# Gated slot attention on Trainium2: the first four steps of a software pipeline in another order

## The reference, cut to what matters

```python
q = _swish((x @ Wq).reshape(b, t, H, K))          # H = 4, K = 32, of layernormed x
k = _swish((x @ Wk).reshape(b, t, H, K))
v = (x @ Wv).reshape(b, t, H, V)
f = jax.nn.log_sigmoid((x @ Wf).reshape(b, t, H, M)) / GATE_LOGIT_NORMALIZER   # M = 64 slots
s = 1.0 - jnp.exp(f)
# per step of the recurrence, ge = exp(f_t):
hk = hk * ge[:, :, None, :] + k_t[..., :, None] * s_t[..., None, :]
logits = jnp.einsum('bhk,bhkm->bhm', q_t * scale, hk)
p = jax.nn.softmax(logits, axis=-1)
hv = hv * ge[..., :, None] + s_t[..., :, None] * v_t[..., None, :]
o_t = jnp.einsum('bhm,bhmv->bhv', p, hv)
...
o = o * jax.lax.rsqrt(jnp.mean(o * o, axis=-1, keepdims=True) + NORM_EPS) * g_norm_w
return o.reshape(b, t, H * V) @ Wo
```

## Time and profile before

| what | value |
|---|---|
| median of 3 runs | 597.54 us (595.57 to 598.49) |
| the profiled execution's own time | 593.18 us |
| span of the profiled execution | 591.4 us |
| PE busy | 530.9 us (90%) |
| DVE busy | 481.9 us (81%) |
| ACT busy | 398.3 us (67%) |
| POOL busy | 355.5 us (60%) |
| mean granted TensorE clock | 0.987 of full |
| the setup and first steps | 0 to about 38 us |
| GSA pipeline at its steady pace | about 38 to 180 us |

### The profile page before, as it was taken

The page is one execution under the profiler, slowest core; times in us unless marked ns, Lnnn a source line. Parts: engine busy times, 40 slices in busy tenths (PEclk is TensorE's granted clock), DMA queues, the critical chain, the costliest instruction groups (busy, mean ns, idle before and its releaser), DMA issues.

```text
span 591.4 us, 17340 instructions
## 1 busy us (share of the span) xinstructions
PE 530.9 (90%) x5328; PEld 408.2 (69%) x5328; DVE 481.9 (81%) x1945; ACT 398.3 (67%) x1033; POOL 355.5 (60%) x362
## 2 busy tenths in 40 slices
PE   4689999999997779999999999999976999999986
PEld 3467677777776547777777777777765778788865
DVE  2578888887877678999999999999988888888862
ACT  2668878878875378988999999999954333333321
POOL 6335555456445898888888888888824433333430
PEclk9899999999999989999999999999989999999999
DMA  6920000000000477888888888888600000000000
GB/s 159 241 37 2 1 1 1 0 0 0 1 1 2 81 130 130 154 154 150 153 153 150 153 151 152 150 154 152 104 2 2 1 19 19 18 18 18 19 18 19
DMA packets 84426, 42.44 MB, mean 72 GB/s; under 512 B 4378, under 2 KB 84132, under 8 KB 84388
## 3 DMA queue, kind: packets, MB, share of 16 engines
q1 hardware_dynamic: 83234, 41.63, 38.5%
q10 hardware_dynamic: 1154, 0.33, 0.2%
HBM read 39.86 MB, written 2.10 MB: 71 GB/s over the span
## 4 chain that ended last, share of the span: by engine, by line
PE 44%; DVE 22%; issue 19%; ACT 5%; POOL 5%; DVEq 1%; POOLq 0%; ACTq 0%
DVE c_P L1044 6%; PE banks L458 5%; PE banks L938 5%; PE banks L925 4%; PE banks L1246 4%; PE banks L891 3%; PE banks L1270 3%; DVE shared L723 3%; PE banks L914 2%; PE banks L449 2%; PE banks L422 2%; PE banks L904 2%; DVE banks L696 2%; DVE shared L702 2%; ACT c_P L972 2%
## 5 line engine op out<-in xcount | busy, mean ns | idle before, releaser
L1138 POOL TENSOR_TENSOR c_bias<-c_fside,c_cm 128x2048 f32<-128x2048 f32 x32 | 146.3, 4571 | 27.3 <-PE banks L891 24.6
L972 ACT ACTIVATE c_P<-c_P,c_min 128x128 f32<-128x128 f32 x512 | 156.6, 391 | 2.4 <-DVE c_min L1044 2.4
L1044 DVE CUSTOM_DVE_ANT_0 c_P<-banks,c_bias 128x128 f32<-128x128 f32 x512 | 116.3, 284 | 5.3 <-PE banks L891 2.3
L925 PE MATMUL banks<-ident,c_P 128*128 128x128 f32 x512 | 74.8, 279 | 6.6 <-DVE shared L1080 5.8
L925 PEld LDWEIGHTS banks<-ident,c_P 128*128 128x128 f32 x512 | 57.9, 142 | 32.9 <-issue 28.4
L1080 DVE COPY shared<-banks 128x512 f32<-128x512 f32 x96 | 65.6, 684 | 0.0
L1246 PE MATMUL banks<-um,lb_s 128*128 128x512 f32 x192 | 55.6, 404 | 2.7 <-ACT shared L1303 1.9
L1482 POOL TENSOR_TENSOR xs<-shared,xs 128x512 fp32r<-128x512 f32 x8 | 10.7, 1334 | 66.5 <-ACT xs L1313 66.5
L1303 ACT ACTIVATE shared<-banks,bi_col 128x512 f32<-128x512 f32 x32 | 22.0, 688 | 38.2 <-PE banks L1246 38.2
L1246 PEld LDWEIGHTS banks<-um,lb_s 128*128 128x128 f32 x192 | 34.2, 188 | 18.9 <-ACT shared L1303 12.5
L1044 DVE DVE_READ_ACCUMULATOR2_ANT c_min<- 128x1 f32 x512 | 42.5, 83 | 0.0
(11 more groups left out here) (195 smaller groups left out, 1295.3 us busy)
## 6 DMA issues: line engine op xcount, KB each, us to landing
c_fside<-in_fside_Bx16xSxS_dram SPq DMA_DIRECT2D x64, 512.0 KB, 7.2
c_ctx<-in_ctx_dram SPq DMA_DIRECT2D x32, 64.0 KB, 5.0
out_dram<-shared SPq DMA_DIRECT2D x8, 256.0 KB, 2.3
X<-in_x_dram SPq DMA_DIRECT2D x3, 512.0 KB, 5.5
kmask_sb<-in_mask_BxS_bf_dram SPq DMA_DIRECT2D x1, 512.0 KB, 7.4
X<-in_x_dram SPq DMA_DIRECT2D x2, 128.0 KB, 3.3
c_P<-in_L_ffn_wi_dram SPq DMA_DIRECT2D x1, 256.0 KB
c_P<-in_L_ffn_lora_B_dram SPq DMA_DIRECT2D x1, 256.0 KB
```

The costliest lines, as they stand in the source:

```text
L925: last = nc.tensor.transpose(bank(2 + i % 2)[:, 128 * j:128 * j + 128], P[:, q, XG * i + j, :], ident[:])
L972: last = nc.scalar.activation(P[:, par, h, :], P[:, par, h, :], ACT.Exp, bias=mn[:, par, h:h + 1], scale=-1.0)
L1044: last = nc.vector.tensor_tensor_reduce(out=P[:, o, h, :], in0=bank(score_banks(n + 1)[i])[:, 128 * j:128 * j + 128], in1=fm[:, o, h, :], ...
L1138: nc.gpsimd.tensor_tensor(fm[:, q, :, :], fs[:, q, :, :], bc(cm[:], XH), ALU.add).then_inc(C["fm"], 1)
```

## The change

The program's instructions are the same ones. The sigmoids of a step get a name of their own ("sigmoids" in place of "gates" of the turn flag, L624), and the calls for steps 1 to 3 are split by names, so that parts of a step stand in another order on ACT, DVE, PE and POOL. Step 0 changes on ACT alone. From step 4 on each engine's order is as before.

```diff
--- before.py
+++ after.py
@@ -621,7 +621,7 @@
                 weights_turned()
             if on(finish, "roots"):
                 root_logs()
-            if on(turn, "gates"):
+            if on(turn, "sigmoids"):
                 sigmoids()
             if on(finish, "roots"):
                 roots()
@@ -1544,7 +1544,10 @@
             gsa_peeled(gsa, 0)
             setup_lora(pool)
             setup_constants(pool)
-            for t in range(1, 6):
+            gsa_peeled(gsa, 1)
+            gsa_peeled(gsa, 2, "roots", "heads")
+            gsa_peeled(gsa, 2, "weights")
+            for t in range(3, 6):
                 gsa_peeled(gsa, t)
             gsa_loop(pool, gsa)
             for t in range(PAIRS - 2, PAIRS):
@@ -1589,10 +1592,20 @@
             setup_loads(act)
             nc.scalar.preload_act_table_set("natural_log_exp_and_others")
             gsa_normalise(act, 0)
-            for t in range(0, 2):
-                gsa_peeled(gsa, t)
+            gsa_peeled(gsa, 0, "inputs", "gates")
+            gsa_normalise(act, 1)
+            gsa_peeled(gsa, 1, "inputs", "sigmoids", "decays", "gates")
+            gsa_normalise(act, 2)
+            gsa_peeled(gsa, 1, "slots")
             act.wait_ge(s_const, 1)
-            for t in range(2, 6):
+            gsa_peeled(gsa, 2, "sigmoids", "inputs", "decays", "normalise")
+            gsa_peeled(gsa, 2, "gates")
+            gsa_peeled(gsa, 2, "exps", "slots")
+            gsa_peeled(gsa, 3, "sigmoids", "inputs")
+            gsa_peeled(gsa, 3, "decays", "normalise", "exps", "gates")
+            gsa_peeled(gsa, 3, "turned")
+            gsa_peeled(gsa, 3, "outputs", "slots")
+            for t in range(4, 6):
                 gsa_peeled(gsa, t)
             gsa_loop(act, gsa)
             for t in range(PAIRS - 2, PAIRS + 1):
@@ -1645,13 +1658,21 @@
             gsa(0, 0, True, False, False, False, False, False)
             dve.wait_ge(s_masks, 1)
             dve.wait_ge(s_x[2], 16)
-            gsa(1, 1, False, True, False, False, False, True)
+            gsa(1, 1, False, True, False, False, False, False, ("silu",))
+            gsa(1, 1, False, True, False, False, False, True, ("statistics", "slots", "values"))
             setup_vector_1(dve)
             gsa(1, 1, True, False, False, False, False, False)
             setup_vector_2(dve)
-            gsa_peeled(gsa, 2)
+            gsa_peeled(gsa, 2, "silu")
+            gsa_peeled(gsa, 2, "attention", "slots")
+            gsa_peeled(gsa, 2, "statistics", "logits", "values")
+            gsa_peeled(gsa, 3, "attention")
+            gsa_peeled(gsa, 2, "gates")
+            gsa_peeled(gsa, 2, "sums")
             dve.wait_ge(s_x[3], 16)
-            gsa_peeled(gsa, 3)
+            gsa_peeled(gsa, 3, "silu")
+            gsa_peeled(gsa, 3, "logits")
+            gsa_peeled(gsa, 3, "statistics", "slots", "mix", "sums", "values", "gates")
             dve.wait_ge(s_x[4], 16)
             dve.wait_ge(s_x[5], 16)
             for t in range(4, 6):
@@ -1714,13 +1735,22 @@
             setup_tensor_1(pe)
             pe.wait_ge(s_masks, 1)
             pe.wait_ge(s_wcopy, 3)
-            gsa_peeled(gsa, 1)
+            gsa_peeled(gsa, 1, "inputs")
+            gsa_peeled(gsa, 1, "decays", "gates", "values", "slots")
             setup_tensor_2(pe)
             pe.wait_ge(s_wcopy, 5)
             pe.wait_ge(s_dconst, 5)
-            gsa_peeled(gsa, 2)
+            gsa_peeled(gsa, 2, "inputs", "attention")
+            gsa_peeled(gsa, 2, "decays", "gates")
+            gsa_peeled(gsa, 2, "values")
+            gsa_peeled(gsa, 2, "logits", "slots")
             pe.wait_ge(s_wcopy, 6)
-            for t in range(3, 6):
+            gsa_peeled(gsa, 3, "attention", "logits")
+            gsa_peeled(gsa, 3, "inputs")
+            gsa_peeled(gsa, 3, "decays", "gates")
+            gsa_peeled(gsa, 3, "turned")
+            gsa_peeled(gsa, 3, "mix", "values", "outputs", "slots")
+            for t in range(4, 6):
                 gsa_peeled(gsa, t)
             gsa_loop(pe, gsa)
             for t in range(PAIRS - 2, PAIRS + 1):
```

## The result

| | before | changed |
|---|---|---|
| median | 596.59 us (594.0 to 598.49, 6 runs) | 603.58 us (601.12 to 605.91, 6 runs) |
| profiled execution's own time | 593.18 us | 603.24 us |
| span | 591.4 us | 601.4 us |
| mean granted clock | 0.987 | 0.964 |
| the mark (L458 of pair 2 starts) | 52.19 us | 60.54 us |

A forecast was written before the change was run, and what follows sets the result against it. A tight exchange of PE and DVE was taken to bound the kernel, the change shifting only the pipeline's fill. Order +2.7 and clock +0.8 made +3.5 us on 597.54: 601.0 us, range 597.5 to 604.0.

The forecast's parts named there:

- rival (c): A second clock fall in loosely filled steps 2 and 3, costing 0.6 to 1.4 us more: 602.4 us; chance 0.20.
- Gate functions first: Step 0 on ACT: pair 0's gate functions precede pair 1's normalising, so L664 starts at 15.6, 2.3 us early.
- I expect no fall of the clock there: PE's idle time before the first decay sums shrinks from 4.1 to some 1.3 us, so its clock stays up.
- The order alone: Late L597 delays mix, mask and what follows, putting the mark at 54.95, +2.7 us without any clock effect.
- The clock in the new gap: PE idles 6.4 us, 41.9 to 48.3, then resumes at half clock: +0.8 us, bounds 0 and +1.5.
- the signs: Expected in the changed profile: L597 at 47 to 48, mark at 55 to 56, full clock at 20 to 22 us.
- The rule on idle gaps: Skill page's rule that idle gaps between matmul bursts throttle PE again; with it +3.5 us, without it +2.7.
- The later stages: From step 4 on the order is unchanged, so everything behind the mark moves one for one, 10.92 us per step.
- The rival on the other side, (a): Copy L597 not late enough to matter, early gates keep their 2.65 us gain: 594.9 us; chance 0.12.
- old slack (5.3 us): Slack before mix L481 and mask L723, 2.8 and 2.5 us, said to absorb L597 if it starts by 42.3.
- step 3: L597 waits behind ACT's normalising, exponentials and gates: copy +7.0 us, mix L481 +4.9, mask L723 +3.4, pair 3's L664 +2.0.

The follow-up runs named there:

- e6: Kernel before with only ACT's part of step 0 changed (gate functions of pair 0 ahead of normalising pair 1); 594.24 us, 0.9954 of before.
- e1: Changed kernel with copy L597 moved back right behind the decays on ACT in step 3; 600.78 us, 1.0056 of before.
- e5: Kernel before with the change in steps 0 and 1 alone, steps 2 and 3 as before; 592.49 us, 0.9928 of before.
- e11: Repeat of e5, the change in steps 0 and 1 alone; 592.82 us, 0.9951 of before.
- e12: Repeat of e6, the kernel before with ACT's part of step 0 alone; 593.74 us, 0.9940 of before.
- e7: Changed kernel with extra unread transposes filling PE's waits in steps 1 to 3, 56 after pair 0's turned weights; 597.70 us, 1.0038 of before.
- e10: Kernel before with the change in steps 2 and 3 alone, steps 0 and 1 as before; 604.58 us, 1.0131 of before.
- e2: Changed kernel with fewer extra unread transposes in PE's waits than e7, 36 in place of 56 in step 3; 601.38 us, 1.0063 of before.
- e8: Changed kernel with both edits: L597 right behind the decays in step 3, and extra transposes in steps 1 to 3; 591.71 us, 0.9932 of before.

## Why the prediction came out as it did

The direction held, and so did the place: L597 behind the gate functions, with L481, L723 and L664 queued behind it. The measured 603.58 is inside the range, near its upper end, but the forecast of +3.5 us was half of the 7.0 that came. That it is inside is in part luck: the range reached 6.5 us above the 597.54 on which it was built, the median of three runs; with six runs before stands at 596.59, and from there the same range would end at 603.05. And it reached so far only because it was drawn past rival (c). Step by step:

- Gate functions first, L664 at 15.6: measured 15.64, 15.63 in e6.
- "I expect no fall of the clock there": wrong for the changed kernel. PE waited 1.68 us for L403 and 0.98 for L411, and the clock was low for 3.4 us from 19.3; it cost 1.7 us, where nothing was put down. It was not a sure fall either: e1, which is the same program up to step 3, did not have it, nor did e5, e6 and e11 with the same start on ACT; e12 had it for 6.8 us. L664 of pair 1 was at 26.16 instead of 24.2; where the clock held, at 24.37 to 24.48.
- The order alone, +2.7: +3.5 by e7. At full clock L597 came at 48.03 (47.7 reckoned), L481 at 48.65 (48.3), L664 of pair 3 at 52.37 (51.8), the mark at 55.66 (54.95). The rests of 0.3 at the copy and 0.4 behind it are sizes, no mechanism.
- "The clock in the new gap", +0.8, with bounds 0 and +1.5: this fall came, and measured 1.4 us, inside the bounds. What failed is that it was the only clock term. Against full clock (e7) the clock cost 4.9 us at the mark: 1.7 for the fall at 19.3, which was expected not to come, 1.8 for the fall at 36.4 in the loosely filled step 2, and 1.4 for the gap. The fall at 36.4 lasted 10.2 us, made L458 take 3.68 us instead of 2.00 and the projections L411 and L413 2.9 instead of 1.9, and so pushed the copy back. That was rival (c), given 0.20 and priced at 0.6 to 1.4. The changed kernel, e1 and e10, all with steps 2 and 3 in the new order and nothing to fill them, had this fall (from 36.4, 34.5 and 37.9 us); e2, e7 and e8, with fillers, did not. The window with 0.80 busy of 2.00 at full clock, which spoke against (c), was one look over 2 us; around it before was busy 2.02 of 3.5 us (36.5 to 40), the changed kernel 1.61 of 3.5 just before its fall. But how loose a stretch is doesn't decide alone: in e6 PE was busy 1.40 of 3.5 us (15.5 to 19) and kept its full clock.
- Of the signs, L597 came at 51.56 instead of 47 to 48, the mark at 60.54 instead of 55 to 56, the clock was not full at 20 to 22 us, and PE waited 4.26 us for L597 instead of some 6, since half clock stretched the work in front of the wait. DVE's wait of some 7 us came (7.68).
- The rule on idle gaps was weighed only for the new gap. What the Trainium skill, page "TensorE: Matmul & The Clock Gate", section "HAM oscillation — how this bites in real kernels", says of idle gaps, that the burst behind one starts cold (at the lower clock), held there: behind 4.26 us of waiting L481 took 2.08 us in the changed kernel, and behind 2.75 us also in e2, instead of 1.16. The section "What's actually happening" of that page of the Trainium skill says that activity releases the throttle. The trace agrees only loosely: PE was busy for 6.5 of 6.5 us from 40.0 to 46.5 and still at half clock, so the release can come late.
- The later stages carried the shift: the span behind the mark was 539.2 us before, and between 539.5 and 541.4 in the eleven experiments and the changed kernel. The spread goes with low clock at 180 to 240 and 430 to 480 us. The profiled execution of before, 3.4 us under its median, had little of it.
- The rival on the other side, (a), fell as such: L597 came long after 45. Its gain exists, but only with the start's half of the change, e5 and e6. Its "old slack (5.3 us)" is also read too large: 2.8 and 2.5 are from start to start, and with the copy (0.6) and the mix (1.1) taken off, 3.6 us of slack are left, the same 3.6 by which the prediction's own step 3 goes from +7.0 at the copy to +3.4 at the mask.

What stays open: what decides, in one and the same program, whether the clock falls at 17 to 19 us (e6 and e12). The experiments show that it happens and what it costs, not when.

## What to carry to other kernels

Where an order is written by hand, moving a group of parts forward moves everything queued behind it back: look for the one instruction that other engines need first (here a 0.57 us copy) and put it ahead of long groups that only feed the next round. A gain at the start of a pipeline is kept only if the later steps don't take it back; the change's steps 0 and 1 alone are 0.5 to 0.7% faster than the kernel before, all of it 1.2% slower. And reckon a loose stretch of PE with its clock, which here fell in the loose stretch ahead of the worst gap and made the copy later still: filling the waits with work that nobody reads gave back 4.9 us at the mark.

## What was not expected of the hardware

The granted clock stayed at 1.2 GHz for 10.2 us at a time (36.4 to 46.6 in the changed kernel, 48.3 to 58.6 in e2), the last 6.5 us of the first with PE busy all the time. Transposes of the identity matrix, with results that nothing reads, kept the clock up (e7, full from 16 to 60 us), at some 0.115 us each back to back. One program has its mark at 48.62 in one execution and at 51.47 in another, by a fall of the clock at one place alone.
